# A state-space scan over four states is issued as two scans of two, in a vision tower with Mamba and mixture of experts

## The reference

```python
dt = jax.nn.softplus(dt_in @ W_dt + b_dt)
A = -jnp.exp(A_log)
dA = jnp.exp(dt[..., None] * A)
dBx = dt[..., None] * Bm[:, :, None, :] * xs[..., None]
...
_, h = jax.lax.associative_scan(comb, (dA, dBx), axis=1)
y = jnp.einsum('blds,bls->bld', h, Cm) + D * xs
```

## Time and profile before

| what | value |
|---|---|
| median of three runs | 8827.63 us (8824.43 to 8831.17) |
| the profiled execution | 8837.69 us, span 8835.9 us |
| busy PE, DVE, ACT, POOL | 80%, 80%, 70%, 9% |
| mean granted TensorE clock | 0.918 of full speed |
| scans on DVE | 512, of 3442 ns each |

### The profile page before, as it was taken

One profiled execution on the slowest core, in us unless ns is written; L12 is line 12 of the kernel. 1 busy time (PEld: TensorE's weight loads), 2 busy tenths in 40 slices (PEclk: granted clock), 3 DMA queues, 4 the chain that ended last, 5 costly groups with the idle time before them and its releaser, 6 DMA issues. The chain is left out here.

```text
span 8835.9 us, 117469 instructions
## 1 busy us (share of the span) xinstructions
PE 7084.8 (80%) x33290; PEld 3962.2 (45%) x33290; DVE 7040.5 (80%) x9195; ACT 6165.8 (70%) x13424; POOL 808.2 (9%) x554
## 2 busy tenths in 40 slices
PE   6777777888888888888888888888888888888661
PEld 3444444444444444444444444444444444444330
DVE  2788888888888888888888888888888888888743
ACT  5766666677777777777777777777777777777434
POOL 0134242400000000000000000000000000000065
PEclk9998888999999999999999999999999999999775
DMA  2333323233333333333333333333333333333356
GB/s 96 110 129 115 116 100 107 102 113 118 117 118 112 117 117 116 112 121 119 118 113 116 116 118 113 117 113 120 113 116 116 117 116 116 114 120 109 129 113 199
DMA packets 282498, 1034.03 MB, mean 117 GB/s; under 512 B 37570, under 2 KB 129526, under 8 KB 273824
## 3 DMA queue, kind: packets, MB, share of 16 engines
q1 hardware_dynamic: 248352, 1009.77, 32.1%
q0 software_dynamic: 33792, 21.18, 1.5%
HBM read 951.57 MB, written 90.94 MB: 118 GB/s over the span
## 5 line engine op out<-in xcount | busy, mean ns | idle before, releaser
L1047 PE MATMUL psS<-KM,Q 128*99 128x394 f32 x4096 | 1712.5, 542 | 310.1 <-ACT PTs L578 227.6
L572 ACT ACTIVATE P<-psS,least_s 99x197 f32<-99x197 f32 x4096 | 1417.3, 434 | 640.7 <-DVE least_s L768 633.0
L843 DVE TENSOR_TENSOR_SCAN hs<-dA,hs 128x1576 f32<-128x1576 f32 x512 | 1762.1, 3442 | 62.2
L768 DVE TENSOR_REDUCE least_s<-psS 99x2 f32<-99x394 f32 x2048 | 1083.7, 560 | 312.1 <-PE psS L1047 290.2
L1054 PE MATMUL psS<-cst,P 99*99 99x99 f32 x8192 | 1077.1, 273 | 255.7 <-ACT P L572 238.6
L1054 PEld LDWEIGHTS psS<-cst,P 99*99 99x99 f32 x8192 | 931.5, 180 | 763.5 <-ACT P L572 588.2
L649 ACT ACTIVATE dA<-dt_,aneg 128x394 f32<-128x394 f32 x2048 | 1211.1, 631 | 28.2 <-DVE hs L843 19.2
L1047 PEld LDWEIGHTS psS<-KM,Q 128*99 128x99 f32 x4096 | 643.2, 178 | 1027.6 <-ACT PTs L578 501.7
L578 ACT ACTIVATE PTs<-psS 99x396 f32<-99x396 f32 x2048 | 969.0, 521 | 104.3 <-PE psS L1054 102.6
L1139 PE MATMUL psY<-hs,cst 128*128 128x394 f32 x2048 | 858.9, 551 | 136.1 <-DVE hs L852 136.1
L829 DVE TENSOR_TENSOR hs<-hs,u 128x1576 f32<-128x1576 f32 x512 | 916.3, 1790 | 52.4 <-DMA hs<-bc_scratch 52.4
(11 more groups left out here) (214 smaller groups left out, 9524.4 us busy)
## 6 DMA issues: line engine op xcount, KB each, us to landing
hs<-bc_scratch SPq DMA_DIRECT2D x512, 788.0 KB, 4.2
cr<-bc_scratch SPq DMA_DIRECT2D x512, 788.0 KB, 5.1
pat<-patches SPq DMA_DIRECT2D x64, 1176.0 KB, 7.6
more_scratch<-zeros SPq DMA_DIRECT2D x64, 197.0 KB, 5.2
rows_scratch<-hs SPq DMA_DIRECT2D x1, 12352.0 KB, 43.7
PTs<-more_scratch SPq DMA_DIRECT2D x24, 512.0 KB, 6.5
sum_scratch<-HW SPq DMA_DIRECT2D x64, 148.5 KB
hs<-rows_scratch SPq DMA_DIRECT2D x24, 386.0 KB, 3.4
```

Of the source, the lines that this page charges most:

```text
L572: last = nc.scalar.activation(P[:, r, b, m, 0:T], psS[0:CT, 2 * r + b, m * T:(m + 1) * T], ACT.Exp, bias=least_s[:, r, b, m:m + 1], scale= ...
L768: nc.vector.tensor_reduce(least_s[:, r, b, :], psS[0:CT, 2 * r + b, 0:2 * T].rearrange("p (e t) -> p e t", e=2), axis=AX, op=ALU.min).then ...
L843: nc.vector.tensor_tensor_scan(h, a, h, 0.0, ALU.mult, ALU.add).then_inc(scan_ready, 1)
L1047: mm(psS[0:CT, 2 * r + b, 0:2 * T].rearrange("p (e t) -> p e t", e=2), Q[:, r, b, q * CT:(q + 1) * CT], KM[:, r, h % 2 * 2:h % 2 * 2 + 2, ...
```

## The change

Each scan unit becomes two, `("scan", g, 0)` and `("scan", g, 1)`, of two states each, with a memset and a wait of its own. ACT signals `da_ready` after every second decay instead of every fourth. The two halves may have other units between them. STAGES and PLACE are new numbers for all engines: the order of stages is nearly the same, places of units differ on PE, ACT and DVE, and SP has its units in the same order as before. A semaphore on which nothing waits (`act_waited`) shares the one of `pool_waited`, which makes room for `scan_begun`.

```diff
-UNITS += [("decay", 1, k) for k in range(QN)] + [("scan", 0), ("load", 2), ("-ys", 1), ("-merge",), ("keep",), ("input", 1)]
+UNITS += [("decay", 1, k) for k in range(QN)] + [("scan", 0, 0), ("scan", 0, 1), ("load", 2), ("-ys", 1), ("-merge",), ("keep",), ("input", 1)]
...
-                    act.wait_ge(da_ready, (i - 1) * QUARTERS + d * HALF + HALF)
+                    act.wait_ge(da_ready, (i - 1) * QUARTERS * 2 + d * QUARTERS + QUARTERS)
...
-                if k == QN - 1:
+                if k % 2:
                     last.then_inc(da_ready, 1)
...
-            def scan(i, g):
-                dve.wait_ge(da_ready, i * QUARTERS + g + 1)
+            def scan(i, g, k):
+                dve.wait_ge(da_ready, (i * QUARTERS + g) * 2 + k + 1)
 
                 back_in_time = g >= QUARTERS // 2
                 first = T - 1 if back_in_time else 0
-                nc.vector.memset(dA[:, g % 2, :, :].rearrange("p n (g t) -> p (n g) t", g=G)[:, :, first:first + 1], 0.0).then_inc(zeroed, 1)
-                dve.wait_ge(zeroed, i * QUARTERS + g + 1)
+                nc.vector.memset(dA[:, g % 2, 2 * k:2 * k + 2, :].rearrange("p n (g t) -> p (n g) t", g=G)[:, :, first:first + 1], 0.0).then_inc(zeroed, 1)
+                dve.wait_ge(zeroed, (i * QUARTERS + g) * 2 + k + 1)
                 dve.wait_ge(mul_done, i * MULS + MUL_IN[g])
-                h = hs[:, g % HBUF, :, :].rearrange("p n t -> p (n t)")
-                a = dA[:, g % 2, :, :].rearrange("p n t -> p (n t)")
+                h = hs[:, g % HBUF, 2 * k:2 * k + 2, :].rearrange("p n t -> p (n t)")
+                a = dA[:, g % 2, 2 * k:2 * k + 2, :].rearrange("p n t -> p (n t)")
                 if back_in_time:
                     h, a = h[:, ::-1], a[:, ::-1]
-                nc.vector.tensor_tensor_scan(h, a, h, 0.0, ALU.mult, ALU.add).then_inc(scan_ready, 1)
+                nc.vector.tensor_tensor_scan(h, a, h, 0.0, ALU.mult, ALU.add).then_inc(scan_ready if k else scan_begun, 1)
```

More of the change, by code:

```diff
@@ L57 @@
 HALF = QUARTERS // 2
[L58 to L61, removed]
+UNITS = [("patch",), ("project", 0, 0), ("-scan", 4, 0), ("-scan", 4, 1), ("project", 0, 1), ("-load", 7), ("-input", 5)]
@@ L62 @@
+UNITS += [("-decay", 6, k) for k in range(QN)] + [("-output", 4), ("sigmoid", 0), ("-scan", 5, 0), ("-scan", 5, 1), ("-half", 4), ("-sum", 4), ("gate", 0), ("-input", 6)]
+UNITS += [("-decay", 7, k) for k in range(QN)] + [("-output", 5), ("xproj", 0), ("share", 0), ("dtproj", 0), ("-scan", 6, 0), ("-scan", 6, 1), ("-half", 5), ("-sum", 5), ("-input", 7)]
+UNITS += [("dt", 0), ("-output", 6), ("load", 0), ("-scan", 7, 0), ("-scan", 7, 1), ("-half", 6), ("-sum", 6)]
 UNITS += [("decay", 0, k) for k in range(QN)] + [("-output", 7), ("load", 1), ("-half", 7), ("-sum", 7), ("input", 0)]
-UNITS += [("decay", 1, k) for k in range(QN)] + [("scan", 0), ("load", 2), ("-ys", 1), ("-merge",), ("keep",), ("input", 1)]
@@ L64 @@
-UNITS += [("decay", 2, k) for k in range(QN)] + [("output", 0), ("-leave",), ("-route",), ("-store",), ("project", 1, 0), ("load", 3), ("scan", 1), ("half", 0), ("sum", 0),
+UNITS += [("decay", 1, k) for k in range(QN)] + [("scan", 0, 0), ("scan", 0, 1), ("load", 2), ("-ys", 1), ("-merge",), ("keep",), ("input", 1)]
+UNITS += [("decay", 2, k) for k in range(QN)] + [("output", 0), ("-leave",), ("-route",), ("-store",), ("project", 1, 0), ("load", 3), ("scan", 1, 0), ("scan", 1, 1), ("half", 0), ("sum", 0),
@@ L65 @@
           ("project", 1, 1), ("input", 2)]
-UNITS += [("decay", 3, k) for k in range(QN)] + [("output", 1), ("sigmoid", 1), ("scan", 2), ("half", 1), ("sum", 1), ("gate", 1), ("input", 3), ("output", 2), ("xproj", 1), ("share", 1),
-          ("dtproj", 1), ("scan", 3), ("half", 2), ("sum", 2), ("dt", 1), ("load", 4), ("output", 3), ("half", 3), ("sum", 3), ("ys", 0)]
+UNITS += [("decay", 3, k) for k in range(QN)] + [("output", 1), ("sigmoid", 1), ("scan", 2, 0), ("scan", 2, 1), ("half", 1), ("sum", 1), ("gate", 1), ("input", 3), ("output", 2), ("xproj", 1), ("share", 1),
+          ("dtproj", 1), ("scan", 3, 0), ("scan", 3, 1), ("half", 2), ("sum", 2), ("dt", 1), ("load", 4), ("output", 3), ("half", 3), ("sum", 3), ("ys", 0)]
@@ L246, in vit_mamba_moe @@
                  "sp_ready scan_ready da_ready mv_ready rstd_ready act_route ht_done h2_ready lg_done gl_ready gm_ready "
-                 "score_ready act_waited xt_done e13_done fin_mv fin_ln fin_rs dve_setup weights_ready h_ready dve_back "
+                 "score_ready xt_done e13_done fin_mv fin_ln fin_rs dve_setup weights_ready h_ready dve_back "
                  "xs_ready dtm_ready dve_waited acc_done zeroed y_done ys_ready m_done dve_route sel_ready pos_done flag_set "
                  "e2_done fin_shift fin_stats pe_waited act_read pe_read pool_read dve_read act_merge dve_merge h_kept "
-                 "u_ready xb_ready e_ready e_sig e_gated win_turned taps_ready taps_done poly_ready ").split()
+                 "u_ready xb_ready e_ready e_sig e_gated win_turned taps_ready taps_done poly_ready scan_begun ").split()
         (open_ready, loaded, patches_loaded, pool_ready, unused_ready, rows_zeroed, rows_stored, more_zeroed,
@@ L259, in vit_mamba_moe @@
          fin_stats, pe_waited, act_read, pe_read, pool_read, dve_read, act_merge, dve_merge, h_kept, u_ready,
-         xb_ready, e_ready, e_sig, e_gated, win_turned, taps_ready, taps_done, poly_ready) = (sem(n) for n in names)
+         xb_ready, e_ready, e_sig, e_gated, win_turned, taps_ready, taps_done, poly_ready, scan_begun) = (sem(n) for n in names)
         pair_names = ("x_ready sq_ready ms_done rs_ready hn_ready kq_done q_ready km_ready v_done v_ready round_done max_done "
```

7 lines of the change are left out of this document (4 added, 3 removed).

## The result

The changed kernel takes 9131.9 us (median of four runs, 9117.7 to 9139.3) where the kernel before took 8826.0 beside it: a ratio of 1.0346, with a 95% interval of 1.0333 to 1.036. It is 306 us slower, and the prediction of 8805 us, with its range up to 8882, was wrong.

What follows compares the result with a forecast made beforehand. No engine was full; DVE was short of work only in places. -0.25 us over 52 passes (-13) and -0.9 over ten routed ones (-9) took 8837.7 to 8815.7; adjusted to the median, 8805 us, range 8742 to 8882.

Steps and rivals of the forecast that it cites:

- The cost of the second instruction: On DVE, each quarter's second memset and half-scan cost 0.25 us more, 2.0 us a pass for eight.
- items 2 and 3: Quarter 6 on DVE: first half-scan fills idle time before the reductions, -1.9 us; later scores give back +0.5.
- item 3: Behind quarter 6, delayed reductions and a decay among ACT's four scores make later work late: +0.5 us a pass.
- the split starves ACT and TensorE: Rival, chance 0.25: at quarter 6 chains wait 1.9 us longer and TensorE loses clock; 1.2 us a pass, 8880 us.
- Item 1: Quarter 4 on DVE: its extra 0.25 us is covered by the 0.58 us wait before L753, -0.25 a pass.
- Item 5: Behind quarter 7: earlier addition shortens TensorE's idle time, four matmuls run faster, load comes earlier: -0.6 us a pass.
- The rival of a late load: Rival, within the starving rival's 0.25: quarter 0's sum delays a load with 2.4 us to spare; each us more costs 62.
- the clock holds: Rival, chance 0.15: the four matmuls ahead of the load run at full clock in every pass, 8750 us.
- costs and gains cancel: Rival, chance 0.18: a larger fixed part per half-scan adds 0.5 us a pass, no change, 8837 us.

Runs made afterwards that it cites:

- e10: Kernel before with only quarter 6 in halves, its first half ahead of the four reductions, and 95 instructions ahead of DVE's loop: 8665.5 us.
- e8: e3 with one number changed: on DVE the first half of quarter 6 stands ahead of the four reductions: 8769.9 us.
- e3: Changed kernel with the old stages and turns, both halves of each quarter back to back, and 88 instructions ahead of DVE's loop: 8858.4 us.
- e17: e1 with one number of ACT's turns changed: the third decay factor of quarter 7 one place earlier, as in the kernel before: 8716.6 us.
- e18: Changed kernel with ScalarE's turns of the kernel before, no instructions added ahead of the loop, stand present: 9056.0 us.
- e2: Kernel before with 45 instructions added ahead of DVE's loop, so that its body reaches into a fourth block: 8865.3 us.
- e1: Changed kernel with 88 instructions added ahead of DVE's loop, so that its body lies in three blocks: 8895.1 us.

## Why the prediction was wrong

The sum was -0.25 us a pass; the measured difference is 306 us, some 5 a pass. By its steps:

- **The cost of the second instruction** was right in size. I had 0.25 us a quarter; the rows of quarter 4 show 0.22, and e10 against e8 comes to 0.23. Its two parts were off and made up for each other: the second memset-to-scan step is 0.10 us and not 0.19, and the two half-scans take 1.75 and 1.72 us from start to start, 0.11 more than one whole scan, where I had taken 0.06. All eight halves together cost only 22 us in e3, as DVE's waits for the merge and the load gave most back.
- **Quarter 6 (items 2 and 3: -1.9, +0.5)** came out in size with the old turns: e8 is 94 us faster than e3, 1.6 us a pass, for that one move, though part of it may be the clock. In the changed kernel the hole is filled too, the four reductions at quarter 6 wait for nothing, but the next three wait 3.5 us a pass.
- **The step that failed in item 3** is that I let ACT's "decay of 0.5 among them" cost its 0.5 us and no more, within the +0.5. In e17 taking this decay out of that place is worth 180 us, 3.0 us a pass. I had the mechanism as the rival "the split starves ACT and TensorE", with TensorE losing clock behind an idle time of over 2 us, and priced it at 1.2 us a pass, 0.7 of it for a gain that shrinks, which leaves 0.5 for the clock; the price was 2.5 times too low. The condition was off as well, as the clock was also down behind waits of 1.55 and 0.7 us. It was also not the split that starved them: e8 has the split, and that projection at full clock in all its passes.
- **A term was missing**: the place of the loop's body. The sum went by work and waits alone. Forty more instructions in DVE's body carried it into a fourth block, and that stand costs 247 us here. No row of the kernel before shows a stand on DVE. But its instruction queue moved 332 packets, 300 of them in the passes of the loop, and ScalarE stood 2.5 us at its own back edge in each of them: one engine's loop was fetched anew already, and DVE's body was about to grow.
- **Item 1 (quarter 4 covered by the wait before L753)** held where there is no stand: in e3 that wait is 0.38 us a pass for 0.58, so 0.20 of the 0.25 is covered. In the changed kernel it is gone, but there the stand just ahead takes it up whole. **Item 5 (-0.6, the load and the clock)** went the other way in the changed kernel: the DMA wait is 51.0 for 39.3 us. The rival of a late load did not come: L830 waits 1.1 us at the longest.
- The rivals "the clock holds" and "costs and gains cancel" did not come either. e17, however, the changed kernel without its two faults, stands at -121 us, further on the fast side than any case that I had given.

So the 306 us are the stand (247) and what is left without it (59); and these 59 are 180 for one decay factor less 121 that halves and turns win. The sizes depend on one another: the stand costs 291 us in e18, where ScalarE's turns are the old ones. What stays open is why the same stand of 2.5 us costs 29 us in one kernel and 291 in another, what in the pass decides whether the clock falls, and what ScalarE's own stand costs.

## What to carry to other kernels

Where a loop is not unrolled, count the instructions of each engine's body before and after an edit, registers and waits too, and look at the instruction queue of the profile: if its packets per pass jump, shift the body by a few dozen instructions ahead of the loop and time it again. Look at it even where nothing has jumped: an engine may stand at its back edge already, with the profile naming another engine as what it waits for. Here shifting DVE's body alone was 247 us, more than any rearrangement of the work. Split an instruction only where a hole is that the half fits: one quarter in halves, with its first half in the hole, won 170 us, all eight with the same hole filled 72, and all eight back to back lost 22. And before work of half a microsecond is put ahead of what TensorE is waiting for, ask what its clock does behind the longer wait; the loss can be several times the work's own length.

## What the runs showed of the hardware

- A DVE loop body of 325 to 365 instructions runs without any fetch when it lies within three blocks of 128, and stands 2.5 to 2.6 us in the mean (3.0 at the longest, in e2) at each back edge when it touches a fourth. Its fetches are five packets of 8.2 KB a pass.
- ScalarE does the same: five packets a pass and 2.4 to 2.7 us between its branch and its next instruction in the kernel before, put down in part to DVE by the profile. Arithmetic that stands first in the body can run meanwhile (e1).
- A memset and the scan that waits for it are 0.19 us apart when a multiply precedes the memset, and 0.10 when another scan does.
- With one decay factor of 0.63 us moved by one place in ACT's order, the mean TensorE clock over the whole kernel went from 0.914 to 0.935.
- TensorE's clock was down behind the same wait of 2.06 us in 15 of 48 passes, behind one of 1.55 in 22 of 46 in e18 and in none of 49 in e17.
